# Score products of the mixing stage in two halves, with four transposes of the next group between them

## The reference

```python
def _mha(x, Wqkv, bqkv, Wo, bo):
    S, B, _ = x.shape
    hd = D // H
    qkv = x @ Wqkv.T + bqkv
    q, k, v = jnp.split(qkv, 3, axis=-1)
    to_heads = lambda t: t.reshape(S, B, H, hd).transpose(1, 2, 0, 3)
    q, k, v = (to_heads(q), to_heads(k), to_heads(v))
    scores = jnp.einsum('bhqd,bhkd->bhqk', q, k) * (1.0 / np.sqrt(hd))
    att = jax.nn.softmax(scores, axis=-1)
    o = jnp.einsum('bhqk,bhkd->bhqd', att, v)
    o = o.transpose(2, 0, 1, 3).reshape(S, B, D)
    return o @ Wo.T + bo
y = _layer_norm(x + _mha(x, Wqkv, bqkv, Wo, bo), g1, be1)
z = _layer_norm(y + _moe(y, Wg, W1, b1, W2, b2), g2, be2)
```

## Time and profile before

| | |
|---|---|
| median of three runs | 1223.05 us |
| all runs | 1222.92, 1223.05, 1227.51 us |
| profiled execution, its own time | 1222.52 us |
| its span, first to last instruction | 1220.8 us |
| mean granted TensorE clock | 0.983 |
| PE busy | 1124.4 us, 92% of the span |
| DVE busy | 727.6 us, 60% |
| ACT busy | 483.6 us, 40% |
| scores L2452, per matmul record | 193 ns median, 1024 records |
| transposes L2408, per matmul record | 273 ns median, 64 records |

### The profile page before, as it was taken

One profiled execution on the slowest core, in us unless ns is written; L12 is line 12 of the kernel. 1 busy time (PEld: TensorE's weight loads), 2 busy tenths in 40 slices (PEclk: granted clock), 3 DMA queues, 4 the chain that ended last, 5 costly groups with the idle time before them and its releaser, 6 DMA issues. The chain is left out here.

```text
span 1220.8 us, 29847 instructions
## 1 busy us (share of the span) xinstructions
PE 1124.4 (92%) x10228; PEld 768.5 (63%) x10237; DVE 727.6 (60%) x2056; ACT 483.6 (40%) x863; POOL 500.4 (41%) x721
## 2 busy tenths in 40 slices
PE   8999999999999999999898889888889999999995
PEld 3545455464554644645554455666657999999994
DVE  4555666757766677565725556554565655656553
ACT  5444454445454545445352233322213333333330
POOL 3334425244252443442432222343243566556664
PEclk9999999999999999999999999998979999999998
DMA  7266654644637345364372132348013111111110
GB/s 222 71 186 160 173 155 115 184 111 121 188 105 210 88 143 163 89 192 136 80 203 74 53 105 88 114 136 290 20 41 103 48 46 52 49 53 52 52 44 7
DMA packets 142614, 137.97 MB, mean 113 GB/s; under 512 B 29512, under 2 KB 135886, under 8 KB 142416
## 3 DMA queue, kind: packets, MB, share of 16 engines
q1 hardware_dynamic: 136944, 124.20, 35.4%
q0 software_dynamic: 5280, 12.66, 3.1%
q10 hardware_dynamic: 320, 0.16, 0.1%
HBM read 49.37 MB, written 50.83 MB: 82 GB/s over the span
## 5 line engine op out<-in xcount | busy, mean ns | idle before, releaser
L970 ACT ACTIVATE probs<-ps_ab 128x512 f32<-128x512 f32 (+2 forms) x352 | 174.5, 537 | 92.4 <-PE ps_ab L1292 36.5
L591 POOL TENSOR_SCALAR_AFFINE_SELECT probs<-probs 128x512 f32<-128x512 f32 x128 | 81.9, 640 | 267.0 <-ACT probs L970 263.0
L2810 PE MATMUL ps_ab<-e_yT,e_w_now 128*128 128x128 f32 x1248 | 145.8, 275 | 0.0
L2810 PEld LDWEIGHTS ps_ab<-e_yT,e_w_now 128*128 128x128 f32 x1248 | 142.5, 192 | 0.1
L2821 PE MATMUL ps_c<-keep_w,e_hT 128*128 x624 | 141.0, 379 | 0.0
L2821 PEld LDWEIGHTS ps_c<-keep_w,e_hT 128*128 128x128 f32 x624 | 115.7, 190 | 14.1
L712 DVE CUSTOM_DVE_ANT_0 ps_ab<-ps_ab,mask_qk 128x256 f32<-128x256 f32 x224 | 88.9, 450 | 18.9 <-PE ps_ab L1261 18.8
L706 DVE TENSOR_REDUCE top<-ps_ab 128x2 f32<-128x512 f32 (+1 forms) x112 | 74.1, 683 | 28.4 <-PE ps_ab L1261 27.5
L2745 DVE TENSOR_SCALAR e_hT<-ps_ab,keep_b 128x128 f32<-128x128 f32 x312 | 84.4, 343 | 7.5 <-PE ps_ab L2810 4.6
L1261 PE MATMUL ps_ab<-k_rows,q_rows 96*128 96x256 bf16 (+1 forms) x512 | 84.5, 260 | 4.6 <-DVE top L712 2.7
L1820 ACT ACTIVATE e_w_now<-keep_w 128x1024 f32 x78 | 78.1, 1049 | 22.2 <-issue 12.3
(11 more groups left out here) (236 smaller groups left out, 2120.8 us busy)
## 6 DMA issues: line engine op xcount, KB each, us to landing
sorted_rows<-filler SPq DMA_DIRECT2D x8, 4290.0 KB, 16.9
q_rows<-parts SPq DMA_DIRECT2D x96, 128.0 KB, 2.4
k_rows<-parts SPq DMA_DIRECT2D x96, 128.0 KB, 2.4
q_rows<-q_parts SPq DMA_DIRECT2D x96, 128.0 KB, 2.4
keep_w<-in_e_w SPq DMA_DIRECT2D x16, 512.0 KB
keep_w<-in_e_w SPq DMA_DIRECT2D x8, 1024.0 KB
e_row<-sorted_rows SPq DMA_DIRECT2D x39, 130.0 KB, 2.1
x_in<-in_x SPq DMA_DIRECT2D x8, 512.0 KB, 3.9
```

What stands on the lines that cost most here:

```text
L591: nc.gpsimd.affine_select(own, own, [[0, TILES], [1, P]], ALU.is_ge, keep_zero, base=0, channel_multiplier=-1).then_inc(probs_cut.sem, 1)
L970: nc.scalar.activation(probs[:, user % 2, lo:lo + width], ps_exp[:, f % 2, 0:width], ACT.Exp).then_inc(exp_done.sem, 1)
L2810: mm = nc.tensor.matmul(ps_h[s][:, f // 4, (f % 4) * P:(f % 4 + 1) * P], w1_now[:, s, k, f * P:(f + 1) * P], yT[:, s, k * P:(k + 1) * P], ...
```

## The change

`features` takes the list of feature halves it shall do, and `scores` is cut into `score_masks` and `score_blocks`. An iteration now makes the products of the first two row tiles, then the four transposes of `xT0`, then the products of the other two row tiles, and then the four transposes of `xT1`. The signal `scores_full` stays at the last product.

```diff
-                def features(n):
-                    for k in range(KD):
+                def features(n, chunks=range(KD)):
+                    for k in chunks:
                         ps = work_claim(pe, n, f"xT{k}")
...
                 def scores(n):
 
+                    score_blocks(n, range(TILES))
+
+                def score_masks(n):
+
                     pe.wait_ge(q_ready.sem, q_ready.count(n, KD))
...
-                    for c in range(TILES):
+
+                def score_blocks(n, tiles):
+
+                    if 0 in tiles:
+                        score_masks(n)
+                    for c in tiles:
                         for tile in range(KD):
...
-                    mm.then_inc(scores_full.sem, 1)
+                    if TILES - 1 in tiles:
+                        mm.then_inc(scores_full.sem, 1)
...
                 def iteration(n, project=True, route=True):
 
-                    scores(n)
+                    score_blocks(n, range(2))
                     if project:
-                        features(n)
+                        features(n, (0,))
+                    score_blocks(n, range(2, TILES))
+                    if project:
+                        features(n, (1,))
                     if route:
                         output(n)
```

## The result

| | before | after |
|---|---|---|
| median of 20 runs each | 1222.88 us | 1228.97 us |
| range | 1220.19 to 1227.51 | 1222.86 to 1232.99 |
| profiled execution, its span | 1220.8 us | 1229.1 us |
| its mean granted clock | 0.983 | 0.980 |

The ratio is 1.0044 with a 95% interval of 1.0032 to 1.0055. That is 5.4 us, 3.9 to 6.7; the two medians themselves lie 6.1 us apart. The forecast was a median of 1229.6, and 0.43 for slower by more than half a per cent against 0.54 for less. The ratio lies just inside the half per cent, though clear of no change.

The account below looks back on a forecast made before the run. DVE's chain from the scores to the first `mix`, not 92% busy PE, decides when the queries start. Delay 3.3 us plus clock falls 3.2 us gave 6.5 us, median 1229.6 us; own range 1227.5 to 1232, 8 in 10 1223.8 to 1234.0.

Parts of the forecast that it names:

- DVE's chain takes over every delay of the scores: From last score products to queries, DVE's 6.32 us chain decides; later scores pass on in full, except iterations 0 and 1.
- The delay of 0.66 us: Four transposes between the product halves make the scores end 0.66 us later, between 0.57 and 0.8; five iterations, 3.3 us.
- Iteration 6 pays as well, through the shift: In iteration 6 the exponential follows DVE's shift by 0.13 us, so this iteration pays 0.66 us too.
- `xT0` meets its claim in time: The moved transposes need ACT's copy of the previous `v1`, done 0.3 us earlier; otherwise up to 0.3 us per iteration.
- The wait before the queries grows to 2.2 us: PE's wait for the first `mix` grows from 1.36 to 2.2 us in iterations 2 to 5, 1.3 in iteration 6.
- The clock falls in two of four, at 1.6 us each: Two of the four longer waits in iterations 2 to 5 are followed by half clock in the queries: 3.2 us.
- The sum of 6.5 us: Delay 3.3 us plus clock falls 3.2 us on the profiled execution, its span going from 1220.8 to 1227.3 us.
- the two terms: The later end of the scores in five iterations, 3.3 us, and clock falls in the queries, 3.2 us.
- rival 3: The existing clock fall behind the wait at 843.67 us goes away, giving back 4.2 us: 1222.2 us; chance 0.08.
- the first: Only the delay of 3.3 us; the clock holds in all four waits before the queries: 1226.4 us; chance 0.28.
- the second: The clock falls in all four waits before the queries at 2.77 us each: 14.4 us, 1237.5 us; chance 0.12 including anything near.
- The fourth rival: The end of the scores does not matter, DVE being busy with earlier ranks until `m_least`: 1223 us, no change; chance 0.06.

Follow-up runs that it names:

- e4: The kernel before with the change in iterations 0 and 1 alone, iterations 2 to 6 as before: 1215.80 us against 1215.57, ratio 1.0003.
- e1: The changed kernel plus eight short matmuls between output projection and queries in iterations 2 to 5: 1226.26 us, ratio 1.0089 to the kernel before.
- e3: The changed kernel with all eight transposes between the two halves of the products: 1226.60 us against 1215.57 for the kernel before, ratio 1.0085.
- a2: The changed kernel unedited, timed again beside the kernel before on another chip: 1227.32 us against 1221.63, ratio 1.0044.
- e10: The changed kernel unedited, a third time: 1230.50 us against 1225.44 for the kernel before, ratio 1.0051.
- e2: The kernel before plus five short matmuls in PE's wait before the queries in iterations 2 to 5: 1222.08 us, ratio 1.0059 to the kernel before.
- e7: The changed kernel with DVE's statistics of the group after next moved behind the two mixes: 1216.57 us, ratio 0.9955 to the kernel before.
- e5: The changed kernel plus two long fp32 matmuls in the wait before the queries in iterations 2 to 5: 1231.33 us, ratio 1.0086 to the kernel before.

## Why the prediction was right, by its own steps

- **DVE's chain takes over every delay of the scores.** Shown: 6.32 us from `m_least` to the queries before and after in iterations 2 to 5, and in e4, where only the iterations with a wait for `x_in` have the change, that wait takes up the delay. In the profile after this cover was thinner than forecast: the waits for `x_in` were 1.16 and 0.25 us and the queries of iteration 1 started 2.0 us later than before, not where they did, because the mixing had begun 3.9 us later.
- **The delay of 0.66 us.** Measured 0.73 in iteration 2, 0.74 by e1 and e4, and 1.17 with eight transposes (e3). The step from the fourth transpose to the products is the one that was guessed at 0.21: four transposes start at 750.67, the products at 751.26, so 0.59 with three steps of 0.117 leaves 0.24. The bounds, 0.57 and 0.80, held. The Trainium skill, TensorEngine Tiling (Array Packing), Key Properties, says that changing the tiling mode drains TensorE. The trace agrees in part: 0.24 lies between the 0.117 of no drain and the 0.27 of a full one. A full drain would have given 4.0 us for five iterations, the rows gave 3.3, and 5 x 0.73 is 3.65.
- **Iteration 6 pays as well, through the shift.** It did: first product 861.68, `m_least` 863.82, 2.14 against 1.41 before. About 0.1 us of it comes back, as the queries follow `m_least` after 5.28 instead of 5.38 us.
- **`xT0` meets its claim in time.** The copy of `v1` ends at 750.27 in iteration 2, the transposes start at 750.67; 0.4 us of cover, where I had 0.3.
- **The wait before the queries grows to 2.2 us.** 2.31 and 2.32 in three of the four iterations, 1.28 in iteration 6 (1.3 said).
- **The clock falls in two of four, at 1.6 us each.** In the profile it fell in two, at 1.70. In a2 and e10 it fell in three of four. Over three profiled executions, eight of the nine waits of 2.3 us lost the clock; the three of iteration 4 were cut to 1.61 to 1.74 us by a standstill of PE and did not. The price was right. The count was luck: "only just longer than 2.08" was too careful a reason for two of four, and what kept the number near two was a standstill that I had not counted.
- **The sum of 6.5 us.** Measured 5.4 (3.9 to 6.7), 5.7 and 5.1. It is high by about a microsecond, which is inside the scatter. That it is not low is luck too. With three falls in a2 and e10 the two terms make 3.65 + 5.1 = 8.75 us, but from the first query of iteration 1 to that of iteration 6 these traces are only 3.99 and 4.40 us longer than the one before. Two things that no term of the forecast covers gave most of it back: the queries of iteration 1 were 1.4 and 1.1 us shorter, and the stretch at 1.2 GHz behind the heads of iteration 5 was gone, which is rival 3. The two together are 5.9 and 5.5 us, a little more than the 4.8 and 4.35 that are missing; the standstills of PE differ as well.

The rows for that are the last transposes of iteration 5 and the mask of iteration 6, first before (the transposes start at 843.67), then in a2, and the granted clock of a2:

```profile
853.96 0.59 PE L2443 MATMUL ps_c<-m_mask_pos,m_ident 128*128 128x256 bf16 x2
```

```profile
853.99 0.55 PE L2503 MATMUL ps_d<-m_identf,m_rows 128*128 128x128 f32 x3 [1.79 <-issue]
...
859.82 0.38 PE L2447 MATMUL ps_c<-m_mask_pos,m_ident 128*128 128x256 bf16 x2
```

```profile
845.80:868.00 22.20, 19.07 (x340) 14.05 (x339) 8.09 (x25) 7.44 (x12) 4.31 (x5) 1.00 0.49 171
```

From the one to the other it takes 10.29 us before and 5.83 in a2, so that stretch was worth 4.5 us; rival 3 had priced it at 4.2. In e10 it takes 5.83 us too, in the first profile after 10.25.

Of the rivals, the first (delay only, 3.3 us) is out by the traces, the second (all four at 2.77) by size. The third did not happen in the first profile, where the half clock of 844.7 to 854.8 in the earlier trace rows is there again at 852.2 to 862:

```profile
852.20:862.00 9.80, 9.80 (x72) 8.04 (x72) 1.56 (x9) 1.19 (x2) 4.00 (x4) 0.50 0.19 66
```

In a2 and e10 its mechanism did happen, beside the two terms and not in their place, so its 1222.2 us did not come. How often the kernel before keeps that stretch is not known, as it has one profile. The fourth rival is out by the 0.73 us.

What stays open: the clock term is told apart in traces of single executions. In the medians it is not, since the matmuls that kept the clock cost time of their own, and the difference of differences (5.7 less 2.2, and 5.1 less 2.9) leaves 2.2 to 3.5 us for everything that the clock does, with a scatter as large as that. Why PE waits with no releaser was not settled. The 4.4 us wait of e2 falls in a time in which the busy share of the DMA engines reads 0.99 to 1.05, which is no proof: in the profile after PE was busy for all of 841 to 848 us with that share at 1.06.

## What to carry to other kernels

Before work is moved ahead of a signal, find who waits for the signal and whether that engine's chain, and not the engine that signals, decides what comes next: here 92% busy PE had 1.36 us of slack, and DVE none from the scores to the first `mix`. Whoever makes a chain longer on one engine also makes the busy engine's wait longer, and a wait of PE that grows from 1.4 to 2.3 us can cost a second time in the clock. The cheaper repair was in the chain itself: moving work that nobody needs soon out of it gave 7.3 us, part of it by the clock. And a fall of the clock that one profile shows may be missing in the next execution of the same kernel, so a sum that rests on such falls should be read from several profiles.

## What the runs showed of the hardware that was not expected

- Waits of PE before the queries, iterations 1 to 6, by length and what the clock did: waits of up to 1.74 us never lost it, 2.31 or 2.32 did in eight of nine, 2.66 and more always did. A fall in the queries of iterations 2 to 5 made them 1.5 to 1.7 us longer.
- Length alone does not decide. Behind the heads of iteration 5 a standstill of 2.08 us (before) and one of 1.97 (after) were followed by 10 us at 1.2 GHz, one of 2.00 in e4 and one of 1.79 in a2 by none, one of 1.79 in e3 by a short one. In e7 the clock was lost behind standstills of only 1.2 us inside the products.
- Twenty more matmuls in PE's list (e2) cost 6.5 us against before, although they stood in PE's waits: PE stood still elsewhere, with no releaser in the trace. Eight long ones (e5) cost 4.0 us against the changed kernel in the medians, and no trace shows where.
- The same kernel before had medians of 1215.6, 1221.6, 1222.9 and 1225.4 us in four groups of runs, two of them (1215.6 and 1225.4) on the same chip. The first group has no profile of that kernel itself, but in the iterations of e4 that are as before PE's standstill of 1.1 us in the products is missing: an iteration takes 24.0 instead of 25.3 us.
- A single step from transposes of 128 x 128 to products of 64 x 32 costs 0.24 us, twice the 0.117 of a step between transposes.
